# Ordering the first norm and projections of a four-stage transformer kernel by batch

## The reference, cut to what matters

```
xn = (x - mean) / sqrt(var + 1e-5)              # per token
q, k, v = xn @ wq.T, xn @ wk.T, xn @ wv.T       # 16 heads of 64
scores = (q @ k.T) / sqrt(64), causal
```

## Time and profile before

| | |
|---|---|
| Profiled execution, its own time | 1251.86 us |
| Its span, first to last instruction | 1250.1 us |
| Mean granted TensorE clock | 0.965 |
| TensorE matmul busy | 1113.9 us, 89% |
| VectorE busy | 862.7 us, 69% |
| ScalarE busy | 814.1 us, 65% |
| GpSimd busy | 349.3 us, 28% |

### The profile page before, as it was taken

How to read it: one execution, slowest core, us unless ns; L and a number is a source line. 1 busy time by engine, 2 the same in 40 slices (tenths; PEclk the granted TensorE clock), 3 DMA queues, 4 the chain that set the end, 5 groups by cost and what they waited for, 6 DMA issues and landing times.

```text
span 1250.1 us, 28179 instructions
## 1 busy us (share of the span) xinstructions
PE 1113.9 (89%) x10202; PEld 846.4 (68%) x10202; DVE 862.7 (69%) x2486; ACT 814.1 (65%) x1915; POOL 349.3 (28%) x345
## 2 busy tenths in 40 slices
PE   3799999999999999999799993987888888888886
PEld 1587878788888878889576661665556556556674
DVE  4565656665656565655433655999999999999863
ACT  2566666666667676650333442998889989989932
POOL 1596464545455555514000302010000000000043
PEclk9899999999999999999699995999999999999998
DMA  3222232222222232200101035030311203110001
GB/s 109 68 58 69 59 85 59 69 75 69 76 68 75 68 76 69 68 19 26 39 26 43 26 86 61 2 39 27 65 15 27 35 6 40 22 20 2 2 1 34
DMA packets 33147, 58.90 MB, mean 47 GB/s; under 512 B 4810, under 2 KB 18018, under 8 KB 33010
## 3 DMA queue, kind: packets, MB, share of 16 engines
q1 hardware_dynamic: 32210, 55.52, 20.0%
q10 hardware_dynamic: 800, 1.57, 0.4%
HBM read 27.59 MB, written 4.33 MB: 26 GB/s over the span
## 4 chain that ended last, share of the span: by engine, by line
PE 55%; DVE 18%; issue 11%; ACT 6%; POOL 5%; DMA 3%; SPq 1%; ACTq 0%; POOLq 0%; DVEq 0%
PE pT L1241 12%; PE pO L1164 12%; PE pS L1202 10%; DVE Zb L918 9%; PE pS L1303 4%; PE pT L1112 4%; DVE Sm L933 3%; PE pT L1316 3%; ACT probs L689 3%; PE pS L1264 2%; PE pT L1116 2%; PE pS L1381 1%; DMA KS<-split 1%; PE pS L1361 1%; ACT PT L669 1%
## 5 line engine op out<-in xcount | busy, mean ns | idle before, releaser
L1241 PE MATMUL pT<-cst,probs 128*128 128x128 f32 x2304 | 367.7, 286 | 53.5 <-ACT probs L689 49.6
L1241 PEld LDWEIGHTS pT<-cst,probs 128*128 128x128 f32 x2304 | 255.6, 142 | 148.0 <-ACT probs L689 99.3
L689 ACT ACTIVATE probs<-probs,nmax 128x128 f32<-128x128 f32 (+7 forms) x256 | 198.7, 776 | 131.9 <-DVE nmax L928 130.9
L669 ACT COPY PT<-pT 128x512 f32<-128x512 f32 (+3 forms) x576 | 263.3, 481 | 15.2 <-PE pT L1241 14.1
L928 DVE CUSTOM_DVE_ANT_0 probs<-pS,causal_wide 128x128 f32<-128x128 f32 (+7 forms) x256 | 192.2, 751 | 92.7 <-PE pS L1202 85.1
L689 ACT ACTIVATE probs<-Sm,nmax 128x128 f32<-128x128 f32 (+7 forms) x256 | 199.5, 779 | 58.5 <-DVE nmax L933 51.4
L1164 PE MATMUL pO<-PT,V 128*64 128x128 f32 (+1 forms) x4608 | 230.9, 278 | 3.9 <-issue 2.0
L918 DVE TENSOR_SCALAR Zb<-pS 128x128 bf16<-128x128 f32 (+7 forms) x256 | 192.8, 753 | 19.4 <-PE pS L1208 19.0
L1164 PEld LDWEIGHTS pO<-PT,V 128*64 128x64 f32 (+1 forms) x4608 | 180.0, 113 | 36.6 <-issue 22.3
L933 DVE CUSTOM_DVE_ANT_0 Sm<-pS,Zb 128x128 f32<-128x128 f32 (+7 forms) x256 | 193.4, 756 | 4.5
L513 POOL TENSOR_TENSOR rstd<-rstd,power 128x4 f32<-128x4 f32 x32 | 32.6, 1017 | 559.0 <-DVE rstd L786 558.9
(11 more groups left out here) (183 smaller groups left out, 1364.3 us busy)
## 6 DMA issues: line engine op xcount, KB each, us to landing
Qs<-Ql SPq DMA_DIRECT2D x32, 256.0 KB, 3.7
Kh<-Kh SPq DMA_DIRECT2D x32, 256.0 KB, 3.4
Kl<-Kl SPq DMA_DIRECT2D x32, 256.0 KB, 4.6
wq_t<-factors SPq DMA_DIRECT2D x32, 256.0 KB, 4.0
QS<-split SPq DMA_DIRECT2D x72, 64.0 KB
KS<-split SPq DMA_DIRECT2D x72, 64.0 KB
w1s<-in_w SPq DMA_DIRECT2D x16, 128.0 KB, 2.2
w2s<-in_w SPq DMA_DIRECT2D x16, 128.0 KB, 2.1
```

The costliest lines, as they stand in the source:

```text
L669: nc.scalar.copy(PT[:, g % 2, h, k0 * P:(k0 + nk) * P], pT[r % TBANKS][:, 0:nk * P])\
L689: nc.scalar.activation(probs[:, i % NPROB, 0:n], src[:, 0:n], ACT.Exp, bias=nmax[:, i % 4:i % 4 + 1], scale=-1.0, accum_out=total).then_in ...
L1241: m = nc.tensor.transpose(pT[r % TBANKS][:, kt * P:(kt + 1) * P], probs[:, item % NPROB, (k0 + kt) * P:(k0 + kt + 1) * P], ident)
```

## The change

The four X loads get a semaphore each. X banks 0 and 1 are loaded first, then the constants and w0, then banks 2 and 3. `stage_order(0)` now gives, batch by batch, the moments of both banks and then the norm of both. VectorE's constants are copied behind the whole norm stage. TensorE waits for the constants' load itself (not for `const_ready`), transposes banks 0 and 1 of tokens, does rounds 0 to 2, then transposes banks 2 and 3, then rounds 3 to 5; before attention it waits for `const_ready` and for all of `xnT`. The transposes go to PSUM banks 7, 3, 0 and 1 (`FIRST_BANKS`), since banks 4 to 6 are those of the rounds. ScalarE copies in the same order: two transposed banks, rounds 0 to 2, two transposed banks, rounds 3 to 5. VectorE's low parts still come behind its norm stage. SP exchanges the halves of batch 0's first projections bank by bank: twelve transfers of 128 KB in place of six of 256 KB, all on SP's queue.

```diff
+FIRST_BANKS = (7, 3, 0, 1)
...
     if k == 0:
+        return [(what, j) for b in range(B) for what in ("x moments", "x norm") for j in range(b * NB // B, (b + 1) * NB // B)]
...
+        def halves_landed(c, b):
+            return 16 * 6 * (c + 1 + (b == 0))
...
+            load_x(0)
+            load_x(1)
             sp.dma_start(cst[:, :], consts).then_inc(ld_c, 16)
             sp.dma_start(w0s[:, :, :], w0[0, :, :, :]).then_inc(ld_w0, 16)
+            load_x(2)
+            load_x(3)
...
-            halves(0, 0)
+            def first_halves():
+                def moved(to, source, j):
+                    cols = slice(j * BANK, (j + 1) * BANK)
+                    for n, (rows, other) in enumerate(((slice(DH0, P), slice(0, DH0)), (slice(0, DH0), slice(DH0, P)))):
+                        sp.dma_start(to[rows, 0, n, cols].bitcast(F32), source(n)[other, cols].bitcast(F32)).then_inc(ld_half[0], 16)
+                for j in range(2):
+                    sp.wait_ge(A[0]["cp_dve"], plan.projected(0, 0, 0, j, "dve"))
+                    moved(Qs, lambda n: Ql[:, 0, :], j)
+                for j in range(2):
+                    sp.wait_ge(A[0]["cp_act"], plan.projected(0, 0, 1, j, "act"))
+                    moved(Kh, lambda n: Kh[:, 0, n, :], j)
+                    sp.wait_ge(A[0]["cp_dve"], plan.projected(0, 0, 1, j, "dve"))
+                    moved(Kl, lambda n: Kl[:, 0, n, :], j)
+            first_halves()
...
-            copies_T(0)
+            def copy_first(j):
+                act.wait_ge(tr_done[0], j + 1)
+                nc.scalar.copy(xnT[:, j * BANK:(j + 1) * BANK], bank[FIRST_BANKS[j]]).then_inc(xnT_ready[0], 1)
+            copy_first(0)
+            copy_first(1)
             for r in range(L[0].ahead):
                 act.wait_ge(A[0]["t"], r + 1)
                 projected(A[0], L[0].rounds[r][1], pT[r % TBANKS][:, :])
+                if r == TBANKS - 1:
+                    copy_first(2)
+                    copy_first(3)
...
+            norm_stage(0, None, None)
             dve.wait_ge(ld_c, 16)
             nc.vector.tensor_copy(identb[:, :], ident)
...
-            norm_stage(0, None, None)
...
-            pe.wait_ge(const_ready, 1)
-            transposes(0)
-            pe.wait_ge(xnT_ready[0], NB)
+            def transpose_first(j):
+                pe.wait_ge(xn_ready[0], j + 1)
+                for t in range(TPB):
+                    m = nc.tensor.transpose(bank[FIRST_BANKS[j]][:, t * P:(t + 1) * P], xn[:, j * TPB + t, :], ident)
+                m.then_inc(tr_done[0], 1)
+            pe.wait_ge(ld_c, 16)
+            transpose_first(0)
+            transpose_first(1)
+            pe.wait_ge(xnT_ready[0], 2)
             pe.wait_ge(ld_w0, 16)
             for r in range(L[0].ahead):
+                if r == TBANKS:
+                    transpose_first(2)
+                    transpose_first(3)
...
+            pe.wait_ge(const_ready, 1)
+            pe.wait_ge(xnT_ready[0], NB)
             attention(0)
```

More of the change, by code:

```diff
@@ L183, in stage_order @@
     x = {"x moments": 2, "x norm": 3} if k == 2 else {"x norm": 1, "x moments": 0}
-    if k == 0 or k == 4:
-        steps = x if k == 0 else {"y moments": 0, "y norm": 1}
+    if k == 0:
+        return [(what, j) for b in range(B) for what in ("x moments", "x norm") for j in range(b * NB // B, (b + 1) * NB // B)]
+    if k == 4:
+        steps = {"y moments": 0, "y norm": 1}
     else:
@@ L310, in build @@
                 pT[0][:, :], pT[1][:, :], pT[2][:, :], pO[:, :]]
-        ld_x, ld_c = sem("ld_x"), sem("ld_c")
+        ld_x, ld_c = [sem(f"ld_x{j}") for j in range(NB)], sem("ld_c")
         ld_w0, ld_w = sem("ld_w0"), sem("ld_w")
@@ L380, in _, with load_x @@
         def _(sp):
-            for j in range(NB):
+            def load_x(j):
                 sp.dma_start(X[:, j * TPB:(j + 1) * TPB, :],
-                             x[j * BANK:(j + 1) * BANK, :].rearrange("(n p) d -> p n d", p=P)).then_inc(ld_x, 16)
+                             x[j * BANK:(j + 1) * BANK, :].rearrange("(n p) d -> p n d", p=P)).then_inc(ld_x[j], 16)
+            load_x(0)
+            load_x(1)
             sp.dma_start(cst[:, :], consts).then_inc(ld_c, 16)
             sp.dma_start(w0s[:, :, :], w0[0, :, :, :]).then_inc(ld_w0, 16)
+            load_x(2)
+            load_x(3)
             for dst, src in ((wfc[:, :, :], w_fc.rearrange("(c p) d -> p c d", p=P)), (wpj[:, :], w_proj),
@@ L809, in norm_stage @@
                         else:
-                            dve.wait_ge(ld_x, 16 * (j + 1))
+                            dve.wait_ge(ld_x[j], 16)
                         moments(k, 1, j, lambda n: X[:, n, :])
@@ L1000, in y_ready @@
                 return lambda j: dve.wait_ge(y_done[k], j + 1)
-            dve.wait_ge(ld_half[0], CH0 * (16 * 6))
-            dve.wait_ge(ld_half[1], CH0 * (16 * 6))
+            dve.wait_ge(ld_half[0], halves_landed(CH0 - 1, 0))
+            dve.wait_ge(ld_half[1], halves_landed(CH0 - 1, 1))
             norm_stage(1, y_tile, y_ready(1))
@@ L1181, in scores @@
                             pe.wait_ge(split_step, 2 * HPC * (plan.split_number(c, b, 1, 1) + 1))
-                        pe.wait_ge(ld_half[b], (c + 1) * (16 * 6))
+                        pe.wait_ge(ld_half[b], halves_landed(c, b))
                     half = i // (plan.per // B)
```

## The result

The changed kernel takes 1236.96 us, the median of four runs (1235.65 to 1239.13); the ratio to the kernel before is 0.9861, 95% interval [0.9836, 0.9885]. Timed again later (E9) the ratio was 0.9874 [0.9848, 0.9900]. Forecast were 1240.1 us and a gain of 15.0. The medians by themselves differ by more, 18.1 us from 1255.08; with a fourth run the kernel before has a median of 1256.55, so such a difference is good to a few us only. The first score now starts at 25.75 us in place of 41.32, 15.6 earlier.

The account below looks back on a forecast made before the run. The opening's serial chain of waits up to the first score was taken as the bound; 5.3 + 3.9 - 1.05 + 5.2 + 1.6 = 15.0 us off 1255.08 gave 1240.1 us, range 1234 to 1247.

Parts of the forecast that it names:

- Start of the norm: Opening, VectorE: no longer waiting for the constants, it starts at about 3.75 instead of 9.04; 5.3 us gained.
- Norm: VectorE's norm of four banks: 10.8 instead of 14.7 us, GpSimd's power overlapping, ending at 14.5; 3.9 us gained.
- Constants behind the norm: VectorE between norm and first Ql: the copies of constants now stand there, paid in full; 1.05 us lost.
- Projections off the path: Batch 0's transposes and projections: hidden by 15.5, Qs of bank 0 at 14.2; norm's end to Ql 5.2 us less.
- Exchange: SP's twelve transfers before the first score: 0.55 us an issue, last landing 2.8, score at 26.3; 1.6 us gained.
- Clock: TensorE around the first score: nothing booked for its clock, 2.4 us put on both ends.
- The whole: Whole kernel: 15.0 us gained in the opening, time 1240.1 us; gain of 12.5 to 16.5 given chance 0.62.
- The last sign: Profile after the change: the distance from first score to end stays 1208.8 us; growth would mean gain given back.
- Dear small transfers: Rival, exchange: each issue takes 1.01 us, gain 11, time 1244; with milder forms chance 0.18.
- Clock that stays high, or issues of 0.46: Rival, opening: first score near 25 and 2.4 us more back, gain 16.5 to 19, time 1237; chance 0.10.
- Gain given back in attention: Rival, attention: slow clock or another wait leaves a gain of 0 to 7, about 1251 us; chance 0.07.
- Transfers that don't overlap: Rival, exchange: twelve pieces each wait for the one ahead, 39 us, slower by 14.8, time 1270; chance 0.03.

Follow-up runs that it names:

- E9: The changed kernel run again with no edit; ratio to the kernel before 0.9874.
- E2: Kernel before with VectorE's constants copied behind the norm, a semaphore per X load, transposes waiting for the constants' load, old load order; ratio to before 0.9955.
- E1: Kernel before with only the norm's order changed: moments of two banks, then norms of two; ratio to before 0.9968.
- E4: Changed kernel with all four banks transposed and copied before the first projection; ratio to the kernel before 0.9920.
- E6: Changed kernel with the four Kh transfers issued from ScalarE's queue instead of SP's; 1236.17 us, one run.
- E8: Changed kernel with five unused 512-column matmuls on TensorE between the last V projection and the first score; ratio to the kernel before 0.9866.
- E3: Kernel before with only the exchange changed, twelve transfers of 128 KB bank by bank instead of six of 256 KB; 1247.66 us, one run.
- E11: Changed kernel with six unused 512-column matmuls on TensorE ahead of the first transpose; 1238.29 us, one run.
- E10: E8 with GpSimd's last ternary block moved behind the next pair's high and low parts, that exchange ahead of SP's spreading; ratio to the kernel before 0.9865.

## Why the prediction was right

- **Start of the norm.** 3.76, forecast 3.75. E2 shows it alone worth 5.2 (5.3 forecast).
- **Norm.** It ended at 13.97, forecast 14.5. A bank's moments took 1.40 (3.76 to 5.16) where I had counted 1.52 with gaps. The overlap with GpSimd was free, as the later norm stage had shown. The Trainium skill's rule of a full block (page "SBUF — State Buffer", section "Who interferes with whom") did not show: the power took 1.04 beside the norm, 1.02 alone. The page ties the block to a two-port mode, and no trace here shows whether the norm took that mode. E1: 4.4 for this part (3.9 forecast).
- **Constants behind the norm.** Paid in full, as forecast: 13.88 to the first Ql at 14.83, 0.95 us.
- **Projections off the path.** Qs of bank 0 was done at 14.06, forecast 14.2, just under the cover of the constants. E4 puts the order of transposes at 4.35 at the first Ql and 4.6 at the score (forecast 5.2, less the 1.05 of constants). The way behind it was mis-sized: Kh of bank 1 was forecast for 21.9 and its Kl for 23.3, and they ended at 19.56 and 20.98. TensorE was faster than forecast behind round 2: the transposes of banks 2 and 3 took 1.04 us together and round 3 took 1.02, where 2.24 and 1.84 had been counted. This did not reach the sum, since SP was still busy with the pieces before (from 17.65 to 23.27 without a pause).
- **Exchange.** Two sizes were off, and it is luck that they nearly cancelled. An issue took 0.64 and not 0.55, since only the first of a row takes 0.46 and the others 0.60, with the gap of 0.04; over nine issues that is 0.8 more. The 0.55 had no row behind it, and the second and third issue of the kernel before (0.60 and 0.61, between those of the earlier trace rows) would have given 0.64. The last landing took 2.30 and not 2.8. From the second low part of Q to the score it was 8.1 (17.65 to 25.75), forecast 8.0. The score came at 25.75, forecast 26.3, and the 0.55 between them are mostly the norm's earlier end. That SP's pace sets the tail was right for one queue; that freeing it would pay (my theory in E6) was wrong, the data rate (262 GB/s with the DMA engines full) stands right behind.
- **Clock.** Nothing was booked and nothing came, with an idle stretch of 5.41 us before the score, a little over the 2 to 5 forecast. E8 prices it: 1.3 at the first GpSimd mark, lost again at 91.
- **The whole.** Forecast 15.0 us from the first score; measured there 15.6, and 17.5 and 15.8 by the two ratios. What the ratios have beyond 15.6 lies within their intervals (about 3 us), and the first attention was no shorter (519.4 and 519.6 against 519.7). The last sign that I had named, 1208.8 us from the first score to the end, was too sharp: it is 1211.5 and 1213.7 in the two executions of the changed kernel. The difference lies in the experts and the second attention, which vary by that much between executions; it is no gain given back.
- **The rivals.** Dear small transfers: out by E3. Clock that stays high, or issues of 0.46: neither came (0.50 before the score, issues of 0.60), though the first ratio alone, 17.5 us, would fall in this rival's range. Gain given back in attention: not in the changed kernel, but it is what happened to the further gain of E8. Transfers that don't overlap: out, twelve landed within 9.4 us of the first issue at 16.24.

## What to carry to other kernels

When an opening is a single chain through in-order queues, cost each part by what is queued ahead of the late consumer on its own engine; the parts here add up to within 0.5 us. Moving a load's wait and small set-up work off the first consumer's queue (5.2 us) was worth as much here as either reordering of the work (4.4 and 4.6). Before you chase the next microsecond, look for the next place where the engine waits for another (91 us here, 65 us behind the opening): in E8 a lead of 1.6 us and a transfer 0.7 slower became there a wait of 1.74, the granted clock fell behind it, and the gain was gone.

## What the runs showed of the hardware that I had not expected

- After a TensorE wait of 1.74 (E8) and 1.72 us (E11) near 91 us the granted clock stood at 0.50 for some us, and the first attention was 1.2 and 2.5 us longer than the changed kernel's 519.4. After waits of 0.69 and 1.08 at the same place it stayed at 1.00, and so it did after the standstill of 1.50 before 101.6 in E10. The profile shows what follows upon what, not why.
- The granted clock printed for the opening, 1.00, is not what TensorE ran at (0.91 us a record in the changed kernel, 0.47 with TensorE kept at work). When the records get faster differs between executions of the same opening (six of them took 4.24 to 5.43 us).
- In pieces of 128 KB the on-chip exchange moved 204 GB/s from SP's queue alone, which is SP's pace of 0.64 us a piece, and 262 with ScalarE's beside it. In pieces of 256 KB SP's queue alone reached 279.
- The last of four on-chip transfers of 256 KB, issued in a row, lands after 4.6 us at most places of attention, but after 5.2 and more at some, and not at the same places in every execution (near 91 us 4.57 in the changed kernel, 5.24 and 5.22 in E8 and E11). The cause is open.
